# Swapping two TensorE bursts in every slot of an attention pipeline

## The reference

```python
q = (x @ Wq + bq).reshape(B, S, 16, 32).transpose(0, 2, 1, 3)      # k and v likewise
scores = einsum('bhqd,bhkd->bhqk', q / sqrt(32), k) + attention_bias   # bias [8,16,512,512], float32
scores = where(src_mask, -inf, scores)
ctx = einsum('bhqk,bhkd->bhqd', softmax(scores), v)
x = x + (ctx.reshape(B, S, 512) @ Wo + bo)
```

## Time and profile before

| | before |
|---|---|
| median of 3 runs | 2577.67 us (2573.52 to 2578.06) |
| the profiled execution, its own time | 2573.42 us |
| its span | 2571.6 us |
| PE busy | 2424.2 us, 94% |
| DVE, ACT, POOL busy | 52%, 38%, 38% |
| mean granted clock of TensorE | 0.973 of full speed |

### The profile page before, as it was taken

One profiled execution on the slowest core, in us unless ns is written; L12 is line 12 of the kernel. 1 busy time (PEld: TensorE's weight loads), 2 busy tenths in 40 slices (PEclk: granted clock), 3 DMA queues, 4 the chain that ended last, 5 costly groups with the idle time before them and its releaser, 6 DMA issues. The chain is left out here.

```text
span 2571.6 us, 44303 instructions
## 1 busy us (share of the span) xinstructions
PE 2424.2 (94%) x16100; PEld 1909.9 (74%) x16100; DVE 1342.5 (52%) x2700; ACT 990.1 (38%) x1977; POOL 982.8 (38%) x806
## 2 busy tenths in 40 slices
PE   5999999999998499999999999998589999999999
PEld 4687787777776367777777777776478888888887
DVE  5354454444444577777677667776433323333322
ACT  3231331331331376766666666666212111211211
POOL 0031431422422367767676667765022012102200
PEclk9999999999999699999999999999789999999999
DMA  5201101101101565555556555553411101110100
GB/s 166 75 17 58 41 16 57 41 16 57 41 1 41 188 185 177 178 190 162 180 166 200 162 173 177 174 171 126 153 56 50 49 0 49 49 49 0 49 33 17
DMA packets 133361, 243.69 MB, mean 95 GB/s; under 512 B 13212, under 2 KB 17452, under 8 KB 133184
## 3 DMA queue, kind: packets, MB, share of 16 engines
q1 hardware_dynamic: 133184, 241.39, 29.1%
HBM read 216.17 MB, written 25.20 MB: 94 GB/s over the span
## 5 line engine op out<-in xcount | busy, mean ns | idle before, releaser
L951 POOL TENSOR_TENSOR at_bias<-at_bias,at_mask 128x512 f32<-128x512 f32 x512 | 590.3, 1179 | 309.5 <-DMA at_bias<-in_fside_Bx16xSxS 270.8
L487 ACT ACTIVATE L_hid<-L_turn,L_b1c 128x512 f32<-128x512 f32 x256 | 176.2, 689 | 982.8 <-PE L_turn L285 977.7
L648 DVE CAST L_hh<-L_hid 128x512 fp32r<-128x512 f32 x256 | 123.6, 483 | 795.5 <-PE L_acc L746 756.8
L283 PE MATMUL L_turn<-L_xth,L_w1h 128*128 128x512 f32 x1024 | 406.5, 397 | 7.7 <-ACT L_hid L487 5.4
L744 PE MATMUL L_acc<-L_w2h,L_hh 128*128 128x512 f32 x1024 | 403.3, 394 | 7.6 <-DVE L_hl L650 7.6
L284 PE MATMUL L_turn<-L_xth,L_w1l 128*128 128x512 f32 x1024 | 400.6, 391 | 0.0
L746 PE MATMUL L_acc<-L_w2l,L_hh 128*128 128x512 f32 x1024 | 400.4, 391 | 0.0
L745 PE MATMUL L_acc<-L_w2h,L_hl 128*128 128x512 f32 x1024 | 400.3, 391 | 0.0
L285 PE MATMUL L_turn<-L_xtl,L_w1h 128*128 128x512 f32 x1024 | 400.0, 391 | 0.0
L982 ACT ACTIVATE at_bias<-at_bias,at_neg_top 128x512 f32<-128x512 f32 x512 | 362.9, 713 | 1.3 <-DVE at_neg_top L1105 1.3
L1105 DVE CUSTOM_DVE_ANT_0 at_bias<-at_score,at_bias 128x512 f32<-128x512 f32 x512 | 332.7, 684 | 50.1 <-PE at_score L1259 25.9
(11 more groups left out here) (206 smaller groups left out, 3036.1 us busy)
## 6 DMA issues: line engine op xcount, KB each, us to landing
at_bias<-in_fside_Bx16xSxS SPq DMA_DIRECT2D x256, 512.0 KB, 3.7
L_xin<-in_x SPq DMA_DIRECT2D x8, 1024.0 KB, 5.4
L_xres<-in_x SPq DMA_DIRECT2D x8, 1024.0 KB, 5.5
at_xin<-x_scratch SPq DMA_DIRECT2D x8, 1024.0 KB, 5.9
at_xres<-x_scratch SPq DMA_DIRECT2D x8, 1024.0 KB, 6.3
L_xin<-x_scratch SPq DMA_DIRECT2D x8, 1024.0 KB, 5.6
L_xres<-x_scratch SPq DMA_DIRECT2D x8, 1024.0 KB, 5.5
x_scratch<-L_xres SPq DMA_DIRECT2D x7, 1024.0 KB, 4.3
```

Of the source, the lines that this page charges most:

```text
L283: nc_mm = pe.matmul(out, ah, bh, start=i == 0, stop=False)
L951: nc.gpsimd.tensor_tensor(tile, tile, mask[:, m % TT, :], ALU.add).then_inc(masked, 1)
```

## The change

In each slot of the PE loop the value burst is issued ahead of the score burst. What is computed, and the order on all other engines, stays as it was. The score burst before the loop and the value burst behind it are not touched.

```diff
@@ -1356,12 +1356,12 @@
             def body(b, odd, first, last):
                 for m in range(BLOCKS):
                     after = following(b, m, last)
-                    if after:
-                        scores(*after)
                     if m:
                         context(b, odd, m - 1, first)
                     elif not first:
                         context(b - 1, 1 - odd, BLOCKS - 1, False)
+                    if after:
+                        scores(*after)
                     for j in range(GROUP):
```

## The result

| | before | after |
|---|---|---|
| median | 2577.86 us (2573.52 to 2580.76, 4 runs) | 2636.82 us (2632.91 to 2645.57, 4 runs) |
| profiled execution, its own time | 2573.42 us | 2632.91 us |
| span | 2571.6 us | 2631.1 us |

The ratio is 1.0233, 95% interval 1.021 to 1.0256: 59 us slower. The forecast was 2623, in a range of 2601 to 2642. Of the 14 us between 2623 and 2636.82, 4 lie in the base (2573.4, one execution, where the median of before is 2577.86) and 10 in the cost of the change.

What follows compares the result with a forecast made beforehand. PE was taken to bound the kernel (94% busy, 97% in the full attention slots); six terms, (a) to (f), summed to 49.1 us on 2573.4, giving 2622.5, stated as 2623, range 2601 to 2642.

Steps and rivals of the forecast that it cites:

- The bound and the mechanism: Attention slots: PE is full (97% busy), and the value burst moved first must wait for DVE's late copy of unit 3.
- (a): 58 ordinary slots with filler: the value burst stalls 0.20 us each for DVE's copy, 11.6 us.
- (b): Slots u = 0: `normalize` and `context_lo` make DVE's copy later, stalls of mean 0.50 to 0.83 us, 13.5 us together.
- (c): Same slots u = 0: the later score add pushes DVE's chain by 0.07 to 0.23 us a slot, 4.0 us together.
- (d): Slots u = 3: DVE's chain with `inverse` overruns slots 11 and 15, 2.8 us; slots 3 and 7 cover it.
- (e): Slot 9: the first filler waits for `turn_lo(3)` behind the later first score add, 1.0 us, 7 times, 7.0 us.
- (f): Slots with nothing beside, first and last batch: PE and DVE wait in line, 5.98 us a slot, together 10.2 us.
- The changeover: Gap from value to score burst, unseen before: taken equal to value to transpose, 0 us, bounds -21 to +21 us.
- the clock rival: New stalls in slots 0, 12 and 9 bring some 14 more clock falls, 27 us, or costlier changeover: 2643 to 2650; chance 0.15.
- The bursts do not commute: Denies the rival that PE had to wait anyway ahead of the value burst, so order is free: 2573 to 2578; chance 0.03.
- the direct stalls alone: Rival: DVE has unseen slack, (c) to (e) vanish and (f) is halved: 2603; chance 0.19 together with a gapless changeover.

Runs made afterwards that it cites:

- the split: The changed kernel with the value burst in two parts, only the last 8 matmuls waiting for the copy of unit 3: 2651.00 us, ratio to before 1.0286.

## Why the prediction was right, step by step

**The bound and the mechanism.** Right. PE was full, and what the slots grew by, 58.5 us, is what the profiled execution grew by, 59.5; the value burst waits for DVE's copy of unit 3, and the split shows that this one wait is the stall.

**(a) the stall of ordinary slots.** Right in place, too small: 0.26 us instead of 0.20. The trail of the burst behind the copy, 0.10 us, had been read at the one place in the earlier trace rows. That burst is one of a block u = 0. After the change the trail is 0.14 or 0.15 in 76 places, all of them bursts of blocks u = 1 to 3, as the ordinary slots have; it is 0.10 in 19, all of blocks u = 0, where `normed` or `v_out` is asked for behind the copy (and 0.34 or 0.35 in six more of block 0). Whether DVE was idle ahead of the copy does not part them: of the 76 it was in 59, while in 17 the copy stood directly behind a score add. Why the further wait goes with another trail is not shown. A value from a place of another kind was carried over, and that makes 0.05 x 58 = 3 us of the miss.

**(b), (c) slots u = 0.** 17.3 for 17.5 us, by errors that cancel: slots 0 grew by 0.89 where 0.70 was expected, slots 12 by 0.65 where it was 0.90, slot 4 by 0.67 for 0.73. The part (c) alone can be read between the full change and the kernel where u = 0 was left as it was: slot 4 0.67 against 0.52, slot 0 0.89 against 0.81, slot 12 0.64 against 0.56, so 0.15, 0.08 and 0.08 for my 0.23, 0.16 and 0.07. Clock falls are in the 17.3 as well, so that the agreement is partly luck: slot 4 of the first batch, behind the slots with nothing beside, grew by 1.54.

**(d) slots u = 3.** 5.8 for 2.8 us. Slots 7 grew by 0.03 to 0.57 though I had them covered, 1.9 us in all. Their length follows the spreading copy of `inverse`. Before, it took 0.43 to 0.70 us there and the slots were 7.44 long (7.00 in the last batch) whatever it took; after, it took 0.43 to 1.20. With 0.43 a slot is 7.47 long, with 0.88 7.69, with 1.03 7.84 and with 1.20 8.02. The longest (before, then after, batch 3; DVE):

```profile
1285.09 0.70 DVE L1121 COPY at_normal<-at_inv 128x512 f32<-128x512 f32 x1
```
```profile
1309.25 1.20 DVE L1121 COPY at_normal<-at_inv 128x512 f32<-128x512 f32 x1
```

So slot 7 has the same chain as slots 11 and 15 and covers the copy only while that is short. Why the copy's time varies is open. Another 1.8 us of the 5.8 lie in the two slots 15 ahead of a new round of the loop (one with a fall of the clock), where I had 0.2 each.

**(e) slot 9.** Right: 1.0 us by the same chain, and 8.4 us came back when `turn_lo(3)` was moved.

**(f) slots with nothing beside.** The loop of 5.98 us measured 6.02 and 6.03. What was missing are mostly the clock falls that its idle pieces bring: 12.6 for 10.2 us in the first profile, 15.0 in the second.

**The changeover.** Right, at the value taken: value to score is 1.01, as value to transpose was. The Trainium skill, "TensorE: Matmul & The Clock Gate", section "Step-by-step: what each phase is for", has weight loads pulled ahead of running matmuls where row groups don't conflict or the load goes to the background buffer; in this trace the score loads were not, and the 21 us that it would have saved did not come. The page's first condition excludes this case, as the value burst fills all rows; whether the second applies no run shows. What is shown is only that it didn't happen.

**The clock.** It was set at nothing in the sum, and as a rival at 14 more falls and 27 us. It is 3 to 5 more falls and at most 5 to 12 us. The rival's count of 7 for the slot behind the transposing of x is not right either: 5 of the 7 falls of before are at slots 8 and 9, and 2 where the loop begins a new round, behind idle pieces of 2.6 and 2.5 us. With (a) and (d) the clock closes the gap between 49 and 59.

**The rivals.** 2636.82 lies just above the forecast's own range, 2610 to 2636, and inside the wider one, which reaches up for the clock rival; that rival's mechanism did happen, at about a third of its count or less (3 to 5 falls for 14). The bursts do not commute, and the direct stalls alone (2603) were too few: slot 9, the later adds and the slots with nothing beside make up about half.

## What to carry to other kernels

When two pieces of work on a full engine can stand in either order, ask which one's input is younger, and let the other go first: here the score burst, whose input is one copy older, was a cover of 0.9 us for a copy that ends 0.1 us too late. Then look at who waits for the piece that moves back, on every engine and in every special slot; about half of the loss lay outside the direct stalls. Where a loop has slots without filler, count them apart: there both engines wait in turn, and the whole move is paid.

## What the runs showed of the hardware

- For these three array shapes a changeover costs by what is left, not by what follows: behind the value burst 1.01 us to the score burst as to the transposes, behind the score burst 0.90 to 0.91 us to either.
- The matmul records of one head of the value burst start 0.109 us apart, whether three other heads run in between or none; a burst whose last head starts late is 0.46 us longer.
- Of the kernel before, 122 of 128 slots repeat between two executions within 0.05 us, and the clock falls in the same slots. Of the kernel after it is 84 of 128, and the falls are partly in other slots, 10 and 12.
- From the end of DVE's copy to the start of the value burst that waited for it: 0.14 to 0.15 us in 76 places, 0.10 us in 19 where the burst asks for a further signal.
- The same spreading copy on DVE (128x512, f32) takes 0.43 to 1.55 us.
- The granted clock went to the lower level, 1.2 GHz, and 10 us windows to 0.83, behind two slots with idle pieces of 1.19 us at a place where it had stayed at 1.00; and idle time of the same sum in slot 8 in two pieces instead of three left 3 falls of 7.
